# Moving the column term of three tiles from VectorE to GpSimd and one rounding of W from ScalarE to VectorE

## The chip, the cores and the metric

The kernel runs on one core of one Trainium2 chip. The metric is the device time of one execution in microseconds (us); lower is better. The core has five engines with instruction queues of their own: TensorE (PE: matrix products, with its weight loads shown as PEld), VectorE (DVE), ScalarE (ACT), GpSimd (POOL) and SyncE (SP), which issues nearly all the DMAs. Each engine takes its own queue in order; they meet at semaphores.

## The reference

The input x is (2, 512, 1024) and the context is (2, 1024, 1024), both float32. Cut to what matters:

```python
def fake_quant(x, s, z):                       # 8 bits, range 0..255
    return (clip(round(x / s + z), 0, 255) - z) * s

x = x + matmul(fake_quant(layernorm(x), s1, z1), fake_quant(ctx, s2, z2))
n = layernorm(x).reshape(-1, 1024)             # 1024 rows
probs = softmax(n @ W_router.T)                # 8 experts
topk_p, topk_i = top_k(probs, 2); topk_p /= sum(topk_p)
h = einsum('nd,erd->ner', n, A_stack) * combine(topk_p, topk_i)   # rank 16 each
x = x + n @ W_base.T + b_base + einsum('ner,eor->no', h, B_stack) * 2
```

## The kernel before, in words

The 1024 rows of x are eight tiles of 128 rows (`T` = 8), tiles 0 to 3 from the first batch and 4 to 7 from the second (`TB` = 4). A tile lies in `xs[:, t, :]` as 128 partitions by 1024 float32, and is changed in place through the whole kernel.

First stage, per tile: VectorE takes the mean and variance of x (`statistics_x`), GpSimd makes the scale and the bias of the quantisation (`scale_x`; VectorE itself for tile 0), VectorE writes the quantised bytes (`quantise_x`, L556). TensorE transposes them (L825), VectorE copies them back (`take_a1t`, L561), and TensorE multiplies with the quantised context (`product`, L840), which ScalarE makes chunk by chunk as the context's DMAs land (L366). Since the bytes carry an offset, the product needs a correction that depends on the column alone, the column term `corr`. TensorE sums the columns of the context (L831), ScalarE turns them into `corr` (`make_corr`, L371, one for each batch). VectorE adds the product to xs (`sum_x1`, L573), and then the column term (`add_corr`, L506, two inputs of 128x1024 in SBUF).

Second stage, per tile: VectorE takes the statistics of the sum (`statistics_y`, L510, L513, L514), GpSimd makes `y_scale` and `y_bias` (`scale_y`, six small operations, L293 to L323), and the normalised rows y are made: for tile 0 by VectorE (`make_first_y`, L518), for tile 1 by GpSimd (`make_y`, L329), for the others by ScalarE. y is kept as a float16 high part and a float16 rest. W is split the same way: its scale comes from its largest magnitude, which ScalarE finds chunk by chunk (L401), VectorE spreads onto a diagonal (`spread_w_peaks`, L581, L582), TensorE spreads over the partitions (L920, after product k = 4 of tile 3), and VectorE turns into `scale_w` (`make_w_scale`, L587, L588, L590). Then ScalarE makes the high parts of the eight chunks of W in order (`split_w`, L412, after which come the high part of y's tile 1 and other splits), and VectorE the low parts (L625). The low part of chunk k frees the slot of the staging ring into which SyncE loads the context chunk 8 + k of the second batch (`load_ctx`, L207, L208).

TensorE's order in the second stage is written out by hand. After product k = 1 of tile 3 it transposes y of tile 0 (L856), after k = 4 comes the spreading of the peaks. Then come the products of tiles 0 and 1 with W's high parts chunk by chunk as they are ready (L889), those with the low parts, the narrow products for the router and A (L868 to L870), the column sums of the second batch with the transposition of the gated values `hc` of tile 1 after its chunk 3 (L862), and the last product of tile 1 (`lora`, L877), which waits for `hct_lo` (`split_hct`, L682). From tile 2 on each tile is narrow products, products with W, the first-stage product of tile t + 2, and `lora`.

VectorE's order is a written list too. Around the change it is, with tiles in brackets: sum (0), quantise (2), (3), copy back (2), column term (0), statistics (0), copy back (3), sum (1), diagonal of A's peaks, y (0), column term (1), statistics (1) with the diagonal of W's peaks between the halves, the scales, the low halves of y (0), sums (2), (3), W's low parts. Near tile 1's gate it is: gate (1), quantise (4), bias (0) (`add_bias`, L691), `hct_lo` (1), output sum (0) (`sum_out`, L697), column term (3).

GpSimd's list is short: fills, `scale_x(1, 2)`, `scale_x(2, 4)`, `scale_y(0)`, `scale_y(1)`, `make_y(1)`, `scale_y(2)` and so on.

Of the kernel before, what the change touches and what calls it, by code (L numbers as in the profile page):

```python
# [6 lines left out]
ALU = mybir.AluOpType  # L7
# [23 lines left out]
def xattn_ffn(nc, x, ctx_kv, quant, w_t, bias, ar_t, b_t, out):  # L31
# [13 lines left out]
    TB = T // B  # L45
# [7 lines left out]
    with ExitStack() as stack:  # L53
# [3 lines left out]
        def sem(name):  # L57
            return stack.enter_context(nc.semaphore(name))

        xs = sb("xs", [P, T, D], F32)  # L60
        stage = sb("stage", [P, RING, D], F32)
# [3 lines left out]
        corr = sb("corr", [P, B, D], F32)  # L65
        bias_sb = sb("bias_sb", [P, D], F32)
        b_raw = sb("b_raw", [P, D], F32)
        w_hi = sb("w_hi", [P, K, D], F16)
# [68 lines left out]
        def ar_bank(t):  # L137
            return 3 if t == 1 else 2

        COLSUM_BANK = 6  # L140
        WARM_BANK = 5
        PEAK_BANK = 4
# [18 lines left out]
        ctx_ready = sem("ctx_ready")  # L161
        stage1_done, x1_summed = sem("stage1_done"), sem("x1_summed")
        colsum_done, corr_ready = sem("colsum_done"), sem("corr_ready")
        x1_ready = sem("x1_ready")
        rows_summed = sem("rows_summed")
        floor_set = sem("floor_set")
        w_peaks, w_diag_ready, peaks_spread, w_scale_ready = (sem(n) for n in ("w_peaks", "w_diag_ready",
# [1 line left out]
        ar_peaks, ar_diag_ready, ar_peaks_read, ar_scale_ready = (  # L169
            sem(n) for n in ("ar_peaks", "ar_diag_ready", "ar_peaks_read", "ar_scale_ready"))  # L170
        ar_hi_ready, ar_lo_ready = sem("ar_hi_ready"), sem("ar_lo_ready")
        w_hi_ready, w_lo_ready = sem("w_hi_ready"), sem("w_lo_ready")
        b_hi_ready, b_lo_ready = sem("b_hi_ready"), sem("b_lo_ready")
        y_measured, pool_step = sem("y_measured"), sem("pool_step")
        y_scaled, y_ready, y_transposed = sem("y_scaled"), sem("y_ready"), sem("y_transposed")
# [12 lines left out]

        def w_staged(k):
            return stage_in[k], 32  # L190

        def yt_hi_landed(t):
            return yt_hi_in[t % 2], 16 * (t // 2)
# [84 lines left out]
        @block.gpsimd  # L278
        def _(pool):
            def fill(tile):  # L280
                return nc.gpsimd.memset(tile.rearrange("p t d -> p (t d)").bitcast(U32), OFFSET_PAIR)

            steps = [0]

            def then(ins):
                steps[0] += 1
                ins.then_inc(pool_step, 1)
                pool.wait_ge(pool_step, steps[0])

            def inverse_root(mv, t):  # L290
                w = slice(t, t + 1)
                whole, guess, part = root[:, 0, w], root[:, 1, w], root[:, 2, w]
                then(nc.gpsimd.tensor_scalar(whole, mv[:, w, 1], EPS, None, ALU.add))  # L293
                then(nc.gpsimd.tensor_tensor(guess, whole, minus_half[:, w], ALU.pow))
                then(nc.gpsimd.tensor_scalar(part, whole, guess, guess, ALU.mult, ALU.mult))
                then(nc.gpsimd.tensor_scalar(part, part, -0.5, 1.5, ALU.mult, ALU.add))
                return guess, part

            def inverse_roots(mv, w):
                whole, guess, part = root[:, 0, w], root[:, 1, w], root[:, 2, w]  # L300
                then(nc.gpsimd.tensor_scalar(whole, mv[:, w, 1], EPS, None, ALU.add))
                then(nc.gpsimd.tensor_tensor(guess, whole, minus_half[:, w], ALU.pow))
                then(nc.gpsimd.tensor_tensor(part, whole, guess, ALU.mult))
                then(nc.gpsimd.tensor_tensor(part, part, guess, ALU.mult))
                then(nc.gpsimd.tensor_scalar(part, part, -0.5, 1.5, ALU.mult, ALU.add))
                then(nc.gpsimd.tensor_tensor(guess, guess, part, ALU.mult))
                return guess

            def scale_x(first, last):
                w = slice(first, last)  # L310
                pool.wait_ge(x_measured, last)
                inverse = inverse_roots(mvx, w)
                then(nc.gpsimd.tensor_scalar(q_scale[:, w], inverse, inv_s[:, 0:1], None, ALU.mult))
                then(nc.gpsimd.tensor_tensor(root[:, 2, w], mvx[:, w, 0], q_scale[:, w], ALU.mult))
                nc.gpsimd.tensor_scalar(q_bias[:, w], root[:, 2, w], -1.0, prm[:, 1:2], ALU.mult,
                                        ALU.add).then_inc(x_scaled, last - first)

            def scale_y(t):
                w = slice(t, t + 1)
                pool.wait_ge(y_measured, t + 1)  # L320
                guess, part = inverse_root(mvy, t)
                then(nc.gpsimd.tensor_scalar(y_scale[:, w], guess, part, Y_SCALE, ALU.mult, ALU.mult))
                nc.gpsimd.tensor_scalar(y_bias[:, w], mvy[:, w, 0], y_scale[:, w], -1.0, ALU.mult,  # L323
                                        ALU.mult).then_inc(y_scaled, 1)

            def make_y(t):
                pool.wait_ge(y_scaled, t + 1)
                pool.wait_ge(y_transposed, t)
                nc.gpsimd.tensor_scalar(y[:, :], xs[:, t, :], y_scale[:, t:t + 1], y_bias[:, t:t + 1], ALU.mult,  # L329
                                        ALU.add).then_inc(y_ready, 1)  # L330

            nc.gpsimd.memset(ident[:, :], 0.0).then_inc(ident_ready, 1)
            pool.wait_ge(ident_ready, 1)
            nc.gpsimd.affine_select(out=ident[:, :], in_=ident[:, :], compare_op=ALU.not_equal, fill=1.0,
                                    base=0, pattern=[[-1, P]], channel_multiplier=1).then_inc(ident_ready, 1)
            then(nc.gpsimd.memset(minus_half[:, :], -0.5))
            fill(a2[:, 4:8, :]).then_inc(a2_filled, 1)
            nc.gpsimd.iota(expert_i[:, :], pattern=[[1, EX]], base=0, channel_multiplier=0).then_inc(iota_ready, 1)
            fill(a1[:, 4:8, :]).then_inc(a1_rest_filled, 1)
            pool.wait_ge(consts_ready, 1)  # L340
            scale_x(1, 2)
            scale_x(2, 4)
            scale_y(0)
            scale_y(1)
            make_y(1)
            scale_y(2)
            scale_x(4, 5)
            scale_y(3)
            for t in range(2, T - 1):
                if t >= 3:  # L350
                    scale_y(t + 1)
                if t + 3 < T:
                    scale_x(t + 3, t + 4)

        @block.scalar
        def _(act):
# [53 lines left out]
            def split_w(k):  # L410
                act.wait_ge(w_scale_ready, 1)
                nc.scalar.activation(w_hi[:, k, :], stage[:, k, :], ACT.Identity,  # L412
                                     scale=scale_w[:, 0:1]).then_inc(w_hi_ready, 1)
# [51 lines left out]
                peak_of_w(k)  # L465
            split_first_yt()
            for k in range(K):
                split_w(k)
            split_yt(1)
            split_ar()  # L470
            split_b()
# [23 lines left out]
        def _(dve):  # L495
# [7 lines left out]
            def add_corr(t):  # L503
                dve.wait_ge(x1_summed, t + 1)
                dve.wait_ge(corr_ready, t // TB + 1)
                nc.vector.tensor_tensor(xs[:, t, :], xs[:, t, :], corr[:, t // TB, :], ALU.add).then_inc(x1_ready, 1)  # L506
                dve.wait_ge(x1_ready, t + 1)

            def first_half_y(t):
                nc.vector.bn_stats(bny[:, t, 0, :], xs[:, t, 0:H])  # L510

            def second_half_y(t):
# [57 lines left out]
            def sum_x1(t):  # L570
                dve.wait_ge(stage1_done, t + 1)
                dve.wait_ge(x_quantised, t + 1)
                nc.vector.scalar_tensor_tensor(  # L573
                    out=xs[:, t, :].rearrange("p (h n) -> p h n", h=NH),
                    in0=ps[:, s1_bank(t):s1_bank(t) + 2, :], scalar=s12,
                    in1=xs[:, t, :].rearrange("p (h n) -> p h n", h=NH),
                    op0=ALU.mult, op1=ALU.add).then_inc(x1_summed, 1)
# [43 lines left out]
                                                   op0=ALU.mult, op1=ALU.subtract).then_inc(ar_lo_ready, 1)  # L621

            def split_w(k):
                dve.wait_ge(w_hi_ready, k + 1)
                nc.vector.scalar_tensor_tensor(out=w_lo[:, k, :], in0=stage[:, k, :], scalar=scale_w[:, 0:1],  # L625
                                               in1=w_hi[:, k, :], op0=ALU.mult,
                                               op1=ALU.subtract).then_inc(w_lo_ready, 1)

            def split_b():
                dve.wait_ge(b_hi_ready, 1)  # L630
# [115 lines left out]
            sum_x1(1)  # L746
            spread_ar_peaks()
            make_first_y()
            add_corr(1)
            first_half_y(1)  # L750
            dve.wait_ge(floor_set, 1)
            spread_w_peaks()
# [3 lines left out]
            split_first_yt()  # L756
            sum_x1(2)
            sum_x1(3)
            for k in range(4):
                split_w(k)  # L760
            split_yt(1)
            split_w(4)
# [1 line left out]
            for k in range(5, K):  # L764
                split_w(k)
            make_undo()
            add_corr(2)
            statistics_y(2)
            gate_tile(0)
            split_b()  # L770
# [2 lines left out]
            make_y_lo(2)  # L773
            gate_tile(1)
            quantise_x(4)
            add_bias(0)
            split_hct(1)
            sum_out(0)
            add_corr(3)
            statistics_y(3)  # L780
            centre_a1t(4)
            gate_tile(2)
# [31 lines left out]
        def _(pe):  # L814
# [108 lines left out]

            pe.wait_ge(ar_peaks_read, 1)
            for k in range(K):
                pe.wait_ge(w_hi_ready, k + 1)
                wide(0, k, False, parts=(0,))
                if k == 0:
                    pe.wait_ge(first_half_lo, 1)
                wide(0, k, False, parts=(2,))  # L930
                if k == 2:
                    pe.wait_ge(yt_lo_ready, 1)
                    transpose_y(1)
# [79 lines left out]
```

## Time and profile before

| | us |
|---|---|
| median of 3 runs (lowest, highest) | 168.48 (168.28, 168.65) |
| profiled execution: its own time | 168.88 |
| profiled execution: span of the trace | 167.1 |
| busy: PE / DVE / ACT / POOL | 155.1 / 127.4 / 72.6 / 37.9 |

The span runs from the first instruction to the last; the profiled execution's own time is 1.8 us longer. PE is busy in 93% of the span. A matmul is pipelined: one of 512 columns is shown with 0.38 us, but in a row of them the next starts 0.216 us later, so that a stall of PE is better read from the starts than from the idle time. A group "x6" in a timeline is six instructions from the first one's start to the last one's end.

### The profile page before, as it was taken

To read this page: it belongs to the slowest core of one execution; us is meant where nothing else is said; L and a number is where in the kernel's file an instruction comes from. 1 tells how busy PE (TensorE), PEld (TensorE's weight loads), DVE (VectorE), ACT (ScalarE), POOL (GpSimd) and SP (SyncE) were. 2 spreads that over 40 slices of the span, in tenths; PEclk is the share of its full clock that TensorE was granted. 3 is DMA by queue.
4 is the path that set the end of the run, shared out by engine and by line. 5 is a ranking of instruction groups with operands and counts; after the bars stand their busy time and mean duration, and the time that the engine had idled before them with its cause. 6 is when DMAs were issued, how large, how long until landed. Compare 5 with 4: busy or idle time off the path is not lost.

```text
span 167.1 us, 2467 instructions
## 1 busy us (share of the span) xinstructions
PE 155.1 (93%) x875; PEld 80.5 (48%) x875; DVE 127.4 (76%) x283; ACT 72.6 (43%) x96; POOL 37.9 (23%) x113
## 2 busy tenths in 40 slices
PE   6858889879999999999999999999999999999990
PEld 3324335425446654644564456445644564555540
DVE  7988668999999989999889875988485828607702
ACT  3266699869999873225005300800080008003000
POOL 8204150343000433040614153125300040000000
PEclk9999999999999999999999999999999999999998
DMA  5999999991798523605430903291327002700311
GB/s 100 367 418 409 412 409 408 408 410 63 218 330 263 201 52 74 177 16 158 95 63 4 234 17 63 48 173 34 63 46 205 4 0 44 209 0 0 129 63 65
DMA packets 23677, 26.94 MB, mean 161 GB/s; under 512 B 17776, under 2 KB 18032, under 8 KB 23664
## 3 DMA queue, kind: packets, MB, share of 16 engines
q1 hardware_dynamic: 23520, 26.78, 50.8%
q8 instruction: 7, 0.11, 0.3%
q14 instruction: 6, 0.05, 0.1%
q10 hardware_dynamic: 144, 0.00, 0.0%
HBM read 18.38 MB, written 4.19 MB: 135 GB/s over the span
## 4 chain that ended last, share of the span: by engine, by line
PE 60%; DVE 12%; DMA 10%; ACT 9%; SPq 3%; issue 2%; POOL 2%; DVEq 0%; POOLq 0%
PE ps L889 37%; PE ps L840 10%; DMA xs<-in_x 7%; PE ps L877 6%; ACT w_hi L412 5%; DMA stage<-in_ctx_kv 3%; DVE w_lo L625 2%; SPq L208 2%; PE ps L868 2%; PE ps L870 2%; PE ps L869 2%; ACT a L366 1%; DVE a L556 1%; DVE ar_lo L619 1%; SPq L203 1%
## 5 line engine op out<-in xcount | busy, mean ns | idle before, releaser
L889 PE MATMUL ps<-w_hi,yt_hi 128*128 128x512 f16 x128 | 38.3, 380 | 0.9 <-ACT w_hi L412 0.9
L889 PE MATMUL ps<-w_hi,yt_lo 128*128 128x512 f16 x128 | 38.2, 379 | 0.0
L889 PE MATMUL ps<-w_lo,yt_hi 128*128 128x512 f16 x128 | 37.2, 379 | 0.0
L840 PE MATMUL ps<-a,a_t 128*128 128x512 f16 x128 | 30.1, 379 | 2.2 <-ACT a L366 0.9
L366 ACT ACTIVATE a<-stage,prm,inv_s 128x1024 uint8<-128x1024 f32 x16 | 19.5, 1241 | 9.5 <-DMA stage<-in_ctx_kv 9.2
L447 ACT ACTIVATE gate<-gate,ar_undo 128x1 f32<-128x1 f32 x8 | 2.4, 295 | 46.5 <-DVE gate L661 46.5
L840 PEld LDWEIGHTS ps<-a,a_t 128*128 128x128 f16 x128 | 12.2, 98 | 16.8 <-ACT a L366 1.4
L889 PEld LDWEIGHTS ps<-w_hi,yt_lo 128*128 128x128 f16 x128 | 12.5, 98 | 15.1 <-DVE yt_lo L638 0.2
L889 PEld LDWEIGHTS ps<-w_lo,yt_hi 128*128 128x128 f16 x128 | 12.5, 98 | 14.1
L889 PEld LDWEIGHTS ps<-w_hi,yt_hi 128*128 128x128 f16 x128 | 11.5, 98 | 15.0 <-issue 2.1
L293 POOL TENSOR_SCALAR root<-mvy 128x1 f32<-128x1 f32 x8 | 1.9, 234 | 57.7 <-DVE mvy L514 57.7
L573 DVE SCALAR_TENSOR_TENSOR xs<-ps,con,xs 128x1024 f32<-128x1024 f32 x8 | 10.1, 1275 | 3.7 <-PE ps L840 3.7
L868 PE MATMUL ps<-ar_hi,yt_hi 128*128 128x136 f16 x64 | 11.7, 223 | 0.0
L869 PE MATMUL ps<-ar_lo,yt_hi 128*128 128x136 f16 x64 | 11.7, 223 | 0.0
L870 PE MATMUL ps<-ar_hi,yt_lo 128*128 128x136 f16 x64 | 11.7, 223 | 0.0
L660 DVE MAX8 top<-ps 128x8 f32<-128x8 f32 x8 | 1.3, 166 | 13.6 <-PE ps L870 13.6
L451 ACT ACTIVATE hct_hi<-ps 128x128 fp32r<-128x128 f32 x8 | 2.2, 277 | 19.2 <-PE ps L862 19.2
L691 DVE SCALAR_TENSOR_TENSOR xs<-xs,row_term,bias_sb 128x1024 f32<-128x1024 f32 x8 | 10.3, 1284 | 0.3
L831 PE MATMUL ps<-a,ones 128*128 128x512 f16 x32 | 8.6, 380 | 1.4 <-ACT a L366 1.4
L625 DVE SCALAR_TENSOR_TENSOR w_lo<-stage,scale_w,w_hi 128x1024 f16<-128x1024 f32 x8 | 9.8, 1278 | 0.0
L506 DVE TENSOR_TENSOR xs<-xs,corr 128x1024 f32<-128x1024 f32 x8 | 9.7, 1218 | 0.0
L697 DVE SCALAR_TENSOR_TENSOR xs<-ps,con,xs 128x1024 f32<-128x1024 f32 x7 | 8.9, 1277 | 0.1
(138 smaller groups left out, 248.1 us busy)
## 6 DMA issues: line engine op xcount, KB each, us to landing
stage<-in_ctx_kv SPq DMA_DIRECT2D x16, 512.0 KB, 5.5
stage<-in_w_t SPq DMA_DIRECT2D x8, 512.0 KB, 13.0
xs<-in_x SPq DMA_DIRECT2D x7, 512.0 KB, 12.0
out_dram<-xs SPq DMA_DIRECT2D x7, 512.0 KB, 3.0
ar_raw<-in_ar_t SPq DMA_DIRECT2D x1, 544.0 KB, 13.7
xs<-in_x SPq DMA_DIRECT2D x2, 256.0 KB, 3.8
b_raw<-in_b_t SPq DMA_DIRECT2D x1, 512.0 KB, 12.5
bias_sb<-in_bias SPq DMA_DIRECT2D x1, 512.0 KB, 13.3
```

What stands on the lines that cost most here:

```text
L366: nc.scalar.activation(low_bytes(a2[:, n % K, :]), stage[:, n % RING, :], ACT.Identity, bias=prm[:, 3:4], scale=inv_s[:, 2:3]).then_inc(ct ...
L506: nc.vector.tensor_tensor(xs[:, t, :], xs[:, t, :], corr[:, t // TB, :], ALU.add).then_inc(x1_ready, 1)
L573: nc.vector.scalar_tensor_tensor(out=xs[:, t, :].rearrange("p (h n) -> p h n", h=NH), in0=ps[:, s1_bank(t):s1_bank(t) + 2, :], scalar=s12, ...
L625: nc.vector.scalar_tensor_tensor(out=w_lo[:, k, :], in0=stage[:, k, :], scalar=scale_w[:, 0:1], in1=w_hi[:, k, :], op0=ALU.mult, op1=ALU.s ...
L691: nc.vector.scalar_tensor_tensor(out=xs[:, t, :], in0=xs[:, t, :], scalar=row_term[:, t:t + 1], in1=bias_sb[:, :], op0=ALU.add, op1=ALU.ad ...
L697: nc.vector.scalar_tensor_tensor(out=xs[:, t, :].rearrange("p (h n) -> p h n", n=H), in0=ps[:, OUT_BANK[t % 2]:OUT_BANK[t % 2] + NH, :], s ...
L840: last = nc.tensor.matmul(ps[:, s1_bank(t) + h, :], a1_t[:, t % 4, k, :], a2[:, k, h * H:(h + 1) * H], start=k == 0, stop=k == K - 1)
L868: nc.tensor.matmul(dst, yt_hi[:, p, k, :], ar_hi[:, k, :], start=k == 0, stop=False)
L869: nc.tensor.matmul(dst, yt_hi[:, p, k, :], ar_lo[:, k, :], start=False, stop=False)
L870: last = nc.tensor.matmul(dst, yt_lo[:, p, k, :], ar_hi[:, k, :], start=False, stop=k == K - 1)
L877: ins = nc.tensor.matmul(ps[:, OUT_BANK[t % 2] + h, :], part[:, :], rhs[:, h * H:(h + 1) * H], start=False, stop=stop and part is hct_lo)
L889: ins = nc.tensor.matmul(ps[:, OUT_BANK[p] + h, :], part, rhs[:, k, h * H:(h + 1) * H], start=k == 0 and i == 0, stop=stop and i == 2)
```

## The change

Three things are changed. GpSimd adds the column term of tiles 1, 2 and 3 (`correct_x`), to x itself, after the tile is quantised and before VectorE adds the product; VectorE's `add_corr` for those tiles goes, and its sums of them wait for the addition. VectorE makes the high part of W's chunk 6 (`round_w`) between the low parts of chunks 1 and 2, and ScalarE leaves that chunk out. In VectorE's list `split_hct(1)` stands ahead of `add_bias(0)`.

```diff
+        def w_hi_made(k):
+            if k == VECTOR_W:                      # VECTOR_W = 6
+                return vector_w_hi_ready, 1
+            return w_hi_ready, k + 1 if k < VECTOR_W else k
...
+            def correct_x(t):                      # GpSimd
+                pool.wait_ge(corr_ready, 1)
+                pool.wait_ge(x_quantised, t + 1)
+                nc.gpsimd.tensor_tensor(xs[:, t, :], xs[:, t, :], corr[:, 0, :], ALU.add).then_inc(x_corrected, 1)
...
             scale_x(2, 4)
+            correct_x(1)
+            correct_x(2)
             scale_y(0)
+            correct_x(3)
             scale_y(1)
             make_y(1)
...
             for k in range(K):                     # ScalarE
-                split_w(k)
+                if k != VECTOR_W:
+                    split_w(k)
...
             def first_half_y(t):                   # VectorE from here on
+                if 0 < t < TB:
+                    dve.wait_ge(x1_summed, t + 1)
...
             def sum_x1(t):
                 dve.wait_ge(stage1_done, t + 1)
                 dve.wait_ge(x_quantised, t + 1)
+                if 0 < t < TB:
+                    dve.wait_ge(x_corrected, t)
...
             def split_w(k):
-                dve.wait_ge(w_hi_ready, k + 1)
+                dve.wait_ge(*w_hi_made(k))
...
+            def round_w(k):
+                dve.wait_ge(w_scale_ready, 1)
+                nc.vector.tensor_scalar(w_hi[:, k, :], stage[:, k, :], scale_w[:, 0:1], None,
+                                        ALU.mult).then_inc(vector_w_hi_ready, 1)
...
             make_first_y()
-            add_corr(1)
             first_half_y(1)
...
-            for k in range(4):
+            for k in range(2):
+                split_w(k)
+            round_w(VECTOR_W)
+            for k in range(2, 4):
                 split_w(k)
...
             make_undo()
-            add_corr(2)
             statistics_y(2)
...
             quantise_x(4)
+            split_hct(1)
             add_bias(0)
-            split_hct(1)
             sum_out(0)
-            add_corr(3)
             statistics_y(3)
...
-                pe.wait_ge(w_hi_ready, k + 1)      # TensorE, products with W's high parts
+                pe.wait_ge(*w_hi_made(k))
```

## Rows read from the trace of the kernel before

**Rows 1.** Windows by stage: window, length, busy time by engine, clock, DMA, GB/s.
```profile
32.00:38.00 6.00, 5.06 (x27) 2.34 (x25) 5.73 (x17) 4.43 (x8) 2.01 (x7) 1.00 1.02 406
62.00:70.00 8.00, 7.62 (x42) 4.28 (x41) 7.64 (x19) 2.82 (x5) 2.28 (x7) 1.00 0.49 97
70.00:160.00 90.00, 90.00 (x518) 47.94 (x516) 64.41 (x144) 21.20 (x34) 18.91 (x57) 1.00 0.34 82
...
165.00:167.00 2.00, 0.00 (x0) 0.00 (x0) 0.00 (x0) 0.00 (x0) 0.00 (x0) 0.81 0.22 70
```
**Rows 2.** The chain that ended last: start, us, what.
```profile
31.55 0.72 DVE y L518
...
35.89 8.43 ACT w_hi L412 x8
...
51.48 5.14 DMA stage<-in_ctx_kv
...
67.61 0.21 DVE hct_lo L682
```
**Rows 3.** Timeline of PE: start, us, engine, line, operation, out<-in, count, idle time.
```profile
32.33 1.09 PE L856 MATMUL ps<-ident,y 128*128 128x128 f32 x8
...
34.63 0.32 PE L920 MATMUL ps<-diag,ones_b 128*128 128x384 bf16 x1
...
59.97 2.32 PE L889 MATMUL ps<-w_lo,yt_hi 128*128 128x512 f16 x10
...
63.53 1.90 PE L831 MATMUL ps<-a,ones 128*128 128x512 f16 x8
65.45 0.33 PE L862 MATMUL ps<-ident,hc 128*128 128x128 f32 x1
65.61 1.89 PE L831 MATMUL ps<-a,ones 128*128 128x512 f16 x8
...
69.37 0.23 PE L868 MATMUL ps<-ar_hi,yt_hi 128*128 128x136 f16 x1
```
**Rows 4.** Timeline of VectorE from the quantisation of tile 2 on.
```profile
23.85 1.54 DVE L556 TENSOR_SCALAR a<-xs,q_scale,q_bias 128x1024 uint8<-128x1024 f32 x2 [0.46 <-POOL q_bias L315]
...
26.05 1.22 DVE L506 TENSOR_TENSOR xs<-xs,corr 128x1024 f32<-128x1024 f32 x1
...
28.62 0.21 DVE L514 BATCH_NORM_AGGREGATE mvy<-bny 128x2 f32<-128x12 f32 x1
...
31.46 0.81 DVE L518 TENSOR_SCALAR y<-xs,y_scale,y_bias 128x1024 f32<-128x1024 f32 x1
...
34.23 0.25 DVE L582 TENSOR_SCALAR diag<-ident,top_w 128x128 bf16<-128x128 f16 x1
...
35.25 0.24 DVE L587 TENSOR_REDUCE power<-ps 128x1 f32<-128x128 f32 x1
```
**Rows 5.** Timeline of GpSimd over the same stretch.
```profile
28.92 0.22 POOL L293 TENSOR_SCALAR root<-mvy 128x1 f32<-128x1 f32 x1 [5.10 <-DVE mvy L514]
...
30.97 0.26 POOL L323 TENSOR_SCALAR y_bias<-mvy,y_scale 128x1 f32<-128x1 f32 x1
...
37.83 1.19 POOL L329 TENSOR_SCALAR y<-xs,y_scale,y_bias 128x1024 f32<-128x1024 f32 x1
```
**Rows 6.** Timeline of ScalarE: the column term of the first batch.
```profile
22.82 1.19 ACT L371 ACTIVATE corr<-ps,con 128x1024 f32<-128x1024 f32 x1
```
**Rows 7.** Timelines of VectorE and GpSimd where the two overlap elsewhere.
```profile
61.68 1.23 DVE L655 TENSOR_TENSOR y_lo<-y,y_hi 128x1024 f16<-128x1024 f32 x1 [0.61 <-ACT y L431]
...
61.94 1.01 POOL L303 TENSOR_TENSOR root<-root 128x1 f32<-128x1 f32 x1
...
114.08 1.32 POOL L315 TENSOR_SCALAR q_bias<-root,prm 128x1 f32<-128x1 f32 x1
```
**Rows 8.** Timelines of VectorE and GpSimd at the start: a cast beside a fill.
```profile
1.57 1.80 POOL L281 MEMSET a<- 128x2048 uint32 x1
...
2.39 1.07 DVE L709 CAST ident<-ident 128x128 f16<-128x128 f32 x1
```

More of the change, by code:

```diff
@@ L138, in ar_bank @@
             return 3 if t == 1 else 2
+        VECTOR_W = 6
         COLSUM_BANK = 6
@@ L163, in xattn_ffn @@
         colsum_done, corr_ready = sem("colsum_done"), sem("corr_ready")
-        x1_ready = sem("x1_ready")
+        x1_ready, x_corrected = sem("x1_ready"), sem("x_corrected")
         rows_summed = sem("rows_summed")
@@ L171, in xattn_ffn @@
         ar_hi_ready, ar_lo_ready = sem("ar_hi_ready"), sem("ar_lo_ready")
-        w_hi_ready, w_lo_ready = sem("w_hi_ready"), sem("w_lo_ready")
+        w_hi_ready, vector_w_hi_ready, w_lo_ready = sem("w_hi_ready"), sem("vector_w_hi_ready"), sem("w_lo_ready")
         b_hi_ready, b_lo_ready = sem("b_hi_ready"), sem("b_lo_ready")
@@ L506, in add_corr @@
                 nc.vector.tensor_tensor(xs[:, t, :], xs[:, t, :], corr[:, t // TB, :], ALU.add).then_inc(x1_ready, 1)
-                dve.wait_ge(x1_ready, t + 1)
+                dve.wait_ge(x1_ready, 1 if t == 0 else t - 2)
             def first_half_y(t):
+                if 0 < t < TB:
+                    dve.wait_ge(x1_summed, t + 1)
                 nc.vector.bn_stats(bny[:, t, 0, :], xs[:, t, 0:H])
```

## The prediction

> **What bounds the kernel now.** I read the windows by stage first [rows 1]. From 70 us to 160 us TensorE is busy in all of 90.00 us at clock 1.00: nothing that frees VectorE can shorten that stretch, and whatever happens earlier only moves its beginning. The time to win or lose lies before 70 us: TensorE has 5.06 us of work in the 6 us from 32 to 38, and 7.62 us in the 8 us from 62 to 70. The chain of waits says who sets these two [rows 2]: y of tile 0 on VectorE, then the high parts of W on ScalarE from 35.89, then a context load that starts at 51.48 when a low part of W has freed its slot, and at last `hct_lo` of tile 1 at 67.61, for which TensorE's `lora` waits.
>
> TensorE's timeline gives the size of the last stall [rows 3]. Before `lora` of tile 0 the last of ten matmuls starts at 59.97 + 9 x 0.216 = 61.91, and the next operation after `lora` starts at 63.53: 1.62 us without a stall. (0.216 is the spacing in a row of matmuls: eight take 1.89 and one is shown with 0.38, so (1.89 - 0.38) / 7.) For tile 1 the last of eight starts at 65.61 + 7 x 0.216 = 67.12 and the next operation at 69.37, which is 2.25 us. So 0.63 us are lost there.
>
> The early chain is read from VectorE's and GpSimd's timelines together [rows 4, 5]. VectorE adds the column term of tile 0 at 26.05 and ends its statistics at 28.83; GpSimd, idle for 5.10 us, makes the scale from 28.92 to 31.23; y of tile 0 is made from 31.46; TensorE transposes it at 32.33 and spreads W's peak at 34.63, which ends at 34.95 [rows 3]; VectorE comes to read it at 35.25.
>
> **The change part by part.**
>
> *The addition on GpSimd.* It takes three additions of 1.22 us [rows 4] off VectorE and gives GpSimd three of the same shape. The trace has no GpSimd addition of this size. The nearest row is its one-input operation on 128x1024, 1.19 us [rows 5]; that is the low end. Twice that, 2.38, is the high end, if both inputs come through one interface after the other. Between them: a small GpSimd operation of the same kind takes 0.26 [rows 5], so 0.93 of the 1.19 is for elements, and with two inputs 0.26 + 2 x 0.93 = 2.1 us. I take 2.1, because the next rows speak for one interface that even VectorE's second input goes through.
>
> The Trainium skill's "GPSIMD Engine Reference", section 3.1, gives 4497 ns for a GpSimd addition of 2048 float32, about twice VectorE's; halved, an estimate of 2.25 us. By it the sum below would be 4.05 instead of 3.6 us.
>
> Where do these additions lie? By the clock alone they fit: the column term is ready at 24.01 [rows 6], and two additions of 2.1 end at 28.2, before GpSimd is wanted at 28.92. But beside them VectorE runs the quantisations of tiles 2 and 3 (23.85 to 25.39) and tile 0's addition. Where VectorE runs an operation with two inputs from SBUF, a GpSimd operation stands still until it is over: a small one of 0.19 us takes 1.01 us beside `y_lo` [rows 7], ending at 62.95 when VectorE's ends at 62.91; one of 0.27 us takes 1.32 us at 114.08; there are four such in the trace. The other direction shows once, less cleanly: a cast of 128x128 on VectorE, 1.07 us where an operation of that size takes 0.25 [rows 4], starts during GpSimd's fill and ends at 3.46, just after the fill's end at 3.37 [rows 8]. I take it that each engine holds the other for a whole instruction.
>
> The Trainium skill's "SBUF — State Buffer", section "Who interferes with whom", says the same as a rule: a VectorE operation with two SBUF inputs, or in a mode that uses both ports, and a GpSimd operation exclude each other, and the second to start blocks fully. The four GpSimd rows agree; that VectorE is held by an addition no row of before shows. Without the rule the sum would be that of the first rival.
>
> With 2.1 us the early chain then goes so. GpSimd's first addition gets in after the quantisations, 25.4 to 27.5. VectorE's addition for tile 0, due at 26.05, waits until 27.5 and ends at 28.7; statistics end 2.78 us after its start as before, at 30.3. GpSimd's second addition, which its list puts ahead of `scale_y(0)`, runs from 28.7 to 30.8. Then the scale, 2.31 us, to 33.1. Behind it in GpSimd's queue stands the third addition, ready to start at once, as VectorE's y is; y is a 128x1024 operation of 0.81 us against 1.22 for the addition, so I count it among those that collide. GpSimd needs no message from another engine for its next instruction, so I let it win: 33.1 to 35.2. y starts at 35.2 instead of 31.46: **+3.75 us**. In a formula, 25.4 + 3 x 2.1 + 1.22 + 2.31.
>
> Behind y nothing gives this back except one thing: without tile 1's column term VectorE is no longer late for the peak. It can read it at the end of TensorE's spreading, 0.30 us sooner relative to it, of which a handover takes 0.05: **-0.25 us**. From the scale of W on VectorE works without a break into W's low parts, so the delay goes through to the context load and to `hct_lo`.
>
> What the new waits hold: `sum_x1(1)` waits for the addition of 27.5, before its turn, with everything of VectorE behind it; `sum_x1(2)` and `(3)` have theirs by 35.2, long before theirs. `first_half_y(1)` waits for a sum that is long done: nothing.
>
> *W's chunk 6 on VectorE.* ScalarE's 8.43 us for eight chunks become 7.4 [rows 2]; its next work is then earlier by 1.05 us, but its later work waits for context loads, so nothing comes of it. VectorE pays one more operation ahead of low parts 2 to 7: 0.73 us, the spacing of the two quantisations (1.54 - 0.81) [rows 4]. Low part 6 frees the slot whose load starts at 51.48, and the load lands later by as much: **+0.73 us** in the gate of tile 1, between 0 (if the load has slack) and 0.81. The column terms of tiles 2 and 3 went from places behind that load, or into TensorE's full stretch: nothing from them.
>
> *`hct_lo` ahead of the bias.* The bias of 1.28 us no longer stands between the gate and `hct_lo`: the 0.63 us stall goes, **-0.63 us**. TensorE already waits a little for `hc` of tile 1, from 65.26 (63.53 + 8 x 0.216) to 65.45 [rows 3]; that wait is the one that is late next and takes the 0.73. Tile 0's output sum ends no later than before; its reader, tile 2's product with W, comes only after narrow products of 1.43 us (24 by 0.06).
>
> The sum: 3.75 - 0.25 + 0.73 - 0.63 = **+3.6 us**. On the profiled execution (span 167.1, own time 168.88, so 1.78 us outside the span, untouched) 172.5; on the median, 0.40 lower, 168.48 + 3.6 = **172.1 us**. With GpSimd's addition at 1.19 the statistics become the later of the two and the sum is +1.3 (169.8); at 2.38 it is +4.5 (173.0). If VectorE's y wins the race at 33.1, y is only 1.65 late, and the sum some 1.8 (170.3). If GpSimd gets in between the two quantisations, at 24.66, VectorE loses more: tile 0's addition goes behind both of GpSimd's, y is 5.4 late, the sum +5.25 (173.7).
>
> **The rivals.**
>
> *The additions fit (not slower).* The place is 24.0 to 28.9 us on GpSimd; the price is nothing, as long as `scale_y(0)` starts by 28.92. It holds if the engines don't hold each other for 128x1024 operations, and additions take under (28.92 - 24.01) / 2 = 2.45 us. For it: GpSimd's 5.10 us of idle time; the cast on VectorE may have waited for something else. Against it: four held GpSimd operations. Then the sum is -0.25 + 0.73 - 0.63 = -0.15, 168.3 us; and where the late load has slack, -0.25 - 0.63 = -0.9, 167.6 us.
>
> *Only GpSimd is held.* It adds from 25.4 to 29.6, the scale ends at 31.9, y starts 0.45 late, the peak is read at 35.4, 0.15 late: with the +0.1 of the rest 168.7 us. For it: all clear rows show this direction.
>
> *The clock falls.* In the forecast TensorE stands idle for most of 3.75 us ahead of y's transposes. The clock is 1.00 in every stretch of work, and 0.81 on average in the last two microseconds, when TensorE has stopped [rows 1]. If it fell to its lower level of 1.2 GHz, the 2.30 us from the transposes to the peak would double: 174.4 us. Against it: that row is an idle end, and here some products of tile 3 divide the wait.
>
> **How the numbers follow.** The forecast, with its orders and lengths of the addition, has 0.57 (its own range 169.8 to 173.7); the clock's fall 0.05; only GpSimd held 0.08; the additions fit 0.30, half of it at 168.3 and half at 167.6. A difference under 0.2%, 0.34 us, can't be told from none, so faster means under 168.14, slower over 168.82. Faster: all of the 167.6 and 0.03 of the 168.3 = 0.18. Same: the remaining 0.12 and 0.03 of the one-sided case = 0.15. Slower: 0.57 + 0.05 + 0.05 = 0.67. The range from 168.1 to 174.0 leaves out the 167.6 case (0.15) and the clock (0.05).
>
> **What would show it.** GpSimd's additions: about 2.1 us apart where free, first at 25.4. VectorE's addition of tile 0: 2.7 us long or starting after 27. The scale of tile 0 from 30.8, y from 35.2, TensorE's L856 at 36, ScalarE's first high part at 39.4. `lora` of tile 1 without a stall before it, and a longer one before `hc`'s transposition. The forecast is wrong if VectorE's addition of tile 0 keeps its 1.22 us at 26.05 beside a running GpSimd addition, or if `scale_y(0)` still starts near 28.9.

## The result, and the profile after

The changed kernel takes 174.92 us in the median of 4 runs (174.54 to 175.49), beside 168.56 us (168.28 to 168.99) for the kernel before: a ratio of 1.0378 with a 95% interval of 1.0341 to 1.0414. It is slower by 6.4 us; forecast were 3.6, with a range up to 174.0. The direction holds, and so does the holding of the two engines by each other; the order in which they take turns and the clock of TensorE do not come as forecast.

The profiled execution has a span of 173.7 us and a time of 175.49 us. Its first stage is a little quicker than that of before by chance of the loads: the last operation of `scale_x(2, 4)` ends at 23.20 us instead of 23.82, and times below are compared from that end where it matters. (Of the twelve traces kept, ten have it at 23.05 to 23.32; that of before and that of `third_after_y` have it at 23.82 and 23.84.) Line numbers are those of the changed kernel: L573 is `quantise_x`, L521 the column term, L535 y of tile 0, L601 the diagonal of W's peaks, L606 and L609 the scale of W, L335 GpSimd's addition.

Windows by stage of the changed kernel: window, length, busy time of PE, PEld, DVE, ACT and POOL, clock, DMA share, GB/s.
```profile
24.00:32.00 8.00, 6.02 (x39) 2.88 (x38) 7.93 (x8) 7.12 (x12) 5.25 (x3) 1.00 1.03 406
32.00:34.00 2.00, 0.42 (x2) 0.22 (x3) 1.80 (x4) 1.29 (x4) 1.53 (x5) 1.00 1.03 410
34.00:41.00 7.00, 4.49 (x16) 2.56 (x15) 4.54 (x6) 1.08 (x2) 4.11 (x7) 0.65 0.58 231
41.00:48.00 7.00, 6.77 (x31) 3.04 (x30) 5.82 (x12) 5.29 (x6) 1.46 (x2) 0.87 0.00 1
...
78.00:166.00 88.00, 88.00 (x497) 46.58 (x496) 62.94 (x141) 21.22 (x34) 19.00 (x57) 1.00 0.34 81
```
The full stretch of TensorE is as full as before [rows 1]; it only begins later. What is new is the clock: 0.65 in the mean from 34 to 41 us, where it was 1.00. In windows of 1 us it is 1.00 up to 36 us, 0.50, that is 1.2 of 2.4 GHz, from 37 to 42, and 1.00 again from 43.

VectorE's timeline of the changed kernel; in square brackets, here and below, the idle time before an operation and what ended it.
```profile
23.23 3.58 DVE L573 TENSOR_SCALAR a<-xs,q_scale,q_bias 128x1024 uint8<-128x1024 f32 x2 [0.47 <-POOL q_bias L321]
...
27.39 2.71 DVE L521 TENSOR_TENSOR xs<-xs,corr 128x1024 f32<-128x1024 f32 x1
30.14 0.69 DVE L527 BATCH_NORM_STATS2 bny<-xs 128x6 f32<-128x512 f32 x1
...
34.25 2.81 DVE L535 TENSOR_SCALAR y<-xs,y_scale,y_bias 128x1024 f32<-128x1024 f32 x1 [0.45 <-POOL y_bias L329]
...
42.01 0.29 DVE L606 TENSOR_REDUCE power<-ps 128x1 f32<-128x128 f32 x1 [3.15 <-PE ps L944]
...
42.52 0.15 DVE L609 TENSOR_SCALAR scale_w<-power 128x1 int32<-128x1 int32 x1
```
GpSimd's timeline over the same stretch, and then its addition by line (least, median and longest ns).
```profile
23.46 5.57 POOL L335 TENSOR_TENSOR xs<-xs,corr 128x1024 f32<-128x1024 f32 x2 [0.26 <-ACT corr L385]
31.77 0.22 POOL L299 TENSOR_SCALAR root<-mvy 128x1 f32<-128x1 f32 x1 [2.74 <-DVE mvy L531]
...
34.17 2.34 POOL L335 TENSOR_TENSOR xs<-xs,corr 128x1024 f32<-128x1024 f32 x1
```
```profile
L335 POOL TENSOR_TENSOR xs<-xs,corr x3: 2342/2801/2802, 23.5 to 34.2; 128x1024 f32<-128x1024 f32 x3
```
Read the two against each other. Free, a GpSimd addition takes 2.34 us; the two that meet a quantisation take 2.80. Two quantisations, 1.54 us before [rows 4], take 3.58; tile 0's column term takes 2.71 instead of 1.22 and ends at 30.10, 1.07 us after GpSimd's second addition ends at 29.03; y takes 2.81 instead of 0.81 and ends at 37.06, 0.55 us after the third addition's end at 36.51. The statistics in between (one input) keep their 0.69.

TensorE's timeline of the changed kernel.
```profile
27.53 2.33 PE L864 MATMUL ps<-a,a_t 128*128 128x512 f16 x10 [1.50 <-DVE a_t L578]
...
33.58 1.02 PE L864 MATMUL ps<-a,a_t 128*128 128x512 f16 x4 [1.98 <-issue]
37.12 1.97 PE L880 MATMUL ps<-ident,y 128*128 128x128 f32 x8 [2.52 <-DVE y L535]
38.88 2.77 PE L864 MATMUL ps<-a,a_t 128*128 128x512 f16 x6
41.44 0.53 PE L944 MATMUL ps<-diag,ones_b 128*128 128x384 bf16 x1
...
72.83 0.33 PE L886 MATMUL ps<-ident,hc 128*128 128x128 f32 x1 [0.71 <-DVE hc L699]
73.00 1.89 PE L855 MATMUL ps<-a,ones 128*128 128x512 f16 x8
...
76.12 0.23 PE L892 MATMUL ps<-ar_hi,yt_hi 128*128 128x136 f16 x1
```
The transposes of y, 1.09 us before [rows 3], take 1.97, and six products 2.77 instead of 1.46: the lower clock. From there to 72.83 nothing is new, and `lora` of tile 1 has lost its stall: from the start of the last column sum (73.00 + 7 x 0.216 = 74.51) to 76.12 it is 1.61 us, where it was 2.25. The wait ahead of the transposition of `hc`, by the starts too, is 72.83 - (70.22 + 8 x 0.216) = 0.88 us, where it was 0.19.

From the end of `scale_x` on, in the traces, the sum is: y ends 37.06 - 23.20 = 13.86 us after it, before 32.27 - 23.82 = 8.45, so **+5.41**; from y's end to the end of the spreading of W's peak 41.97 - 37.06 = 4.91 instead of 2.68, **+2.23**; the peak is read 0.04 instead of 0.30 after that, and its reading takes 0.66 instead of 0.60, **-0.20**; from W's scale to tile 2's narrow products 33.45 instead of 33.52, **-0.07**. That is 7.4; the quicker first stage takes 0.6 and the end 0.15 off it, which leaves the 6.6 by which the span grew. The medians differ by 6.4.

### The profile page after: what moved, and what is told of

Same layout as the page of the kernel before. It is cut to its first block, busy times and chain, and to the rows that moved or that the text cites. A ratio compares the mean times of both kernels' runs of the same rounds, so it can differ in the third digit from the quotient of the medians.

```text
span 173.7 us, 2468 instructions
## 1 busy us (share of the span) xinstructions
PE 157.4 (91%) x875; PEld 81.9 (47%) x875; DVE 130.0 (75%) x281; ACT 71.7 (41%) x95; POOL 46.1 (27%) x116
## 4 chain that ended last, share of the span: by engine, by line
PE 59%; DVE 18%; DMA 10%; SPq 3%; issue 3%; ACT 3%; POOL 3%; DVEq 0%; POOLq 0%
PE ps L913 36%; PE ps L864 9%; DMA xs<-in_x 7%; PE ps L901 6%; DVE w_lo L644 5%; DMA stage<-in_ctx_kv 3%; SPq L214 2%; PE ps L892 2%; PE ps L893 2%; PE ps L894 2%; DVE y L535 2%; DVE xs L521 2%; ACT a L380 1%; DVE xs L592 1%; PE ps L880 1%
## 5 line engine op out<-in xcount | busy, mean ns | idle before, releaser
L864 PE MATMUL ps<-a,a_t 128*128 128x512 f16 x128 | 32.1, 396 | 4.2 <-issue 2.0
L592 DVE SCALAR_TENSOR_TENSOR xs<-ps,con,xs 128x1024 f32<-128x1024 f32 x8 | 10.1, 1274 | 4.0 <-PE ps L864 4.0
L573 DVE TENSOR_SCALAR a<-xs,q_scale,q_bias 128x1024 uint8<-128x1024 f32 x8 | 8.5, 1069 | 3.1 <-POOL q_bias L321 3.0
L307 POOL TENSOR_SCALAR root<-mvx 128x1 f32<-128x1 f32 (+1 forms) x6 | 1.4, 229 | 33.4 <-DVE mvx L547 33.4
```

The source lines that it names most:

```text
L573: nc.vector.tensor_scalar(low_bytes(a1[:, t, :]), xs[:, t, :], q_scale[:, t:t + 1], q_bias[:, t:t + 1], ALU.mult, ALU.add).then_inc(x_quan ...
L592: nc.vector.scalar_tensor_tensor(out=xs[:, t, :].rearrange("p (h n) -> p h n", h=NH), in0=ps[:, s1_bank(t):s1_bank(t) + 2, :], scalar=s12, ...
L864: last = nc.tensor.matmul(ps[:, s1_bank(t) + h, :], a1_t[:, t % 4, k, :], a2[:, k, h * H:(h + 1) * H], start=k == 0, stop=k == K - 1)
```

## The experiments

The theory: a GpSimd addition and a VectorE operation that uses the same way into SBUF hold each other for a whole instruction; y of tile 0 is late by that; TensorE's waits let its clock fall; the rest of the change is worth little. The rivals: the new waits on data, GpSimd's queue alone, the rounding on VectorE, or the clock alone. Each ratio is against the kernel before, run beside it (168.60 to 168.76 us).

**Which part costs.** `no_pool_add` is the changed kernel without GpSimd's additions and the waits for them, `pool_add_only` the kernel before with them alone.
```diff
-            correct_x(1)                  # no_pool_add, against the changed kernel
-            correct_x(2)
             scale_y(0)
-            correct_x(3)
...
-                if 0 < t < TB:
-                    dve.wait_ge(x_corrected, t)
...
+            add_corr(1)                   # so too add_corr(2) and add_corr(3), at their old places
```


> The change without GpSimd's additions: VectorE keeps all its column terms, W's chunk 6 is still made by VectorE and hct_lo stands ahead of the bias. My theory (the additions hold VectorE and then let TensorE's clock fall; the rest of the change is worth little): 168.4 us, between 167.9 and 168.7, by +0.73 for the rounding and -0.63 for hct_lo. Rival (the rounding on VectorE or the new order is what costs): above 170.

Measured: 168.47 us, ratio 0.9987 (0.9972 to 1.0001).

```diff
-                if k != VECTOR_W:         # pool_add_only, against the changed kernel
-                    split_w(k)
+                split_w(k)
...
-            round_w(VECTOR_W)
...
+            add_bias(0)
             split_hct(1)
-            add_bias(0)
```


> Only GpSimd's additions, with their waits; W is split by ScalarE alone and hct_lo stays behind the bias. My theory: all of the loss is here, 174.8 us (174 to 175.5), and the clock falls as in the changed kernel. Rival (loss shared with the rounding): 171 to 173.

Measured: 175.45 us, ratio 1.0421 (1.0392 to 1.0449). Windows of its trace:
```profile
32.00:38.00 6.00, 2.06 (x9) 0.74 0.99 394
38.00:46.00 8.00, 7.30 (x27) 0.76 0.02 8
```
(Here PE alone is shown: busy, clock, DMA share, GB/s.) All of the loss is in the additions with their waits, and with them the fall of the clock. Without them the change is worth 0.1 us, which its interval does not tell from nothing.

**Holding, or waiting for data.** In `spare_adds` nothing of the kernel before is taken away and no instruction gets a new operand; only GpSimd adds the column term to itself into a spare tile.
```diff
             scale_x(2, 4)
+            spare_add(1)      # after corr_ready and x_quantised, as correct_x
+            spare_add(2)
             scale_y(0)
+            spare_add(3)      # nc.gpsimd.tensor_tensor(spare[:, t - 1, :], corr[:, 0, :], corr[:, 0, :], ALU.add)
```


> The kernel before, unchanged but for three more additions on GpSimd at the changed kernel's places: the column term plus itself into a spare tile that nobody reads or waits for. No data of the kernel depends on them. My theory (a GpSimd addition holds VectorE's quantisation, addition and y while it runs, and is held by them): the same delays as in the changed kernel, two quantisations in about 3.6 us, tile 0's addition and y of tile 0 at some 2.7 us each, the clock falls, 174.9 us (174.2 to 175.8). Rival (the new waits on data cost the time, and GpSimd's queue ahead of scale_y(0) a little): 168.6 to 169.5, with those operations at 1.54, 1.22 and 0.81 us.

Measured: 174.36 us, ratio 1.0336 (1.0319 to 1.0353). VectorE's timeline in its trace:
```profile
23.27 3.11 DVE L565 TENSOR_SCALAR a<-xs,q_scale,q_bias 128x1024 uint8<-128x1024 f32 x2 [0.46 <-POOL q_bias L316]
...
26.96 2.25 DVE L515 TENSOR_TENSOR xs<-xs,corr 128x1024 f32<-128x1024 f32 x1
...
33.35 2.36 DVE L527 TENSOR_SCALAR y<-xs,y_scale,y_bias 128x1024 f32<-128x1024 f32 x1 [0.44 <-POOL y_bias L324]
```
The same three operations are long, by 1.0 to 1.6 us each, though nothing waits for the sums that GpSimd makes: VectorE is held. The additions themselves are shorter here, 1.89 us free (the same tile is both inputs; why that is quicker was not tried), which fits the smaller loss. The profiled execution, at 172.33 us the quickest of five, kept its clock at 1.00; the other four, 174.0 to 174.7, have mean clocks of 0.977 to 0.99. Whether the clock makes that difference of 1.7 to 2.4 us is not shown: a mean of 0.99 can come from elsewhere, as in the trace of `no_pool_add` (0.989), which has 0.79 from 12 to 20 us and 1.00 from 20 on.

**The third addition and y.**
```diff
             def correct_x(t):
                 pool.wait_ge(corr_ready, 1)
                 pool.wait_ge(x_quantised, t + 1)
+                if t == 3:
+                    pool.wait_ge(y_ready, 1)
```


> The changed kernel, with GpSimd's third addition made to wait until VectorE has made y of tile 0. My theory: y takes 0.81 instead of 2.81 us and all that follows comes 2.0 us earlier: 172.9 us with the clock still at the lower level when y is transposed, 170.6 if it is at 1.00 there (TensorE's waits before tile 2's and tile 3's products are untouched by this). Rival (y is late for another reason): 174.9.

Measured: 172.49 us, ratio 1.0230 (1.0209 to 1.0250). VectorE, then GpSimd, in its trace:
```profile
34.88 0.81 DVE L537 TENSOR_SCALAR y<-xs,y_scale,y_bias 128x1024 f32<-128x1024 f32 x1 [0.44 <-POOL y_bias L329]
35.61 0.69 DVE L529 BATCH_NORM_STATS2 bny<-xs 128x6 f32<-128x512 f32 x1
...
36.39 1.89 DVE L603 TENSOR_SCALAR diag<-ident,top_w 128x128 bf16<-128x128 f16 x1
```
```profile
35.87 2.36 POOL L337 TENSOR_TENSOR xs<-xs,corr 128x1024 f32<-128x1024 f32 x1 [1.02 <-DVE y L537]
```
y is back at 0.81 us. The addition now lies beside two operations of VectorE: the statistics keep their 0.69 us, but the small diagonal of W's peaks, 0.25 us before [rows 4], takes 1.89 and ends at 38.28, just after the addition's end at 38.23. That is the cleanest row for the holding of VectorE. The clock stayed at 1.00 in this trace, though the two earlier waits of TensorE (1.51 and 1.98 us) are there as in the changed kernel. The time lies between my two cases: the clock's loss is gone, but the held diagonal takes some of the gain back. In the trace y ends 35.69 - 23.84 = 11.85 us after `scale_x`, 3.40 late, and from there to the end of the peak's spreading it is 3.06 instead of 2.68, 0.38 more; together 3.8, and the kernel is 3.7 us slower than before. The held diagonal is thus only 0.4 of the 1.9 us above my 170.6. For the rest, 170.6 was reckoned down from the changed kernel's median, which is 1.0 less than the terms of its trace add up to; why that is so stays open.

**The order in GpSimd's queue.**
```diff
+                if t >= 2:
+                    pool.wait_ge(y_ready, 1)
...
             correct_x(1)
+            scale_y(0)
             correct_x(2)
-            scale_y(0)
             correct_x(3)
```


> The changed kernel, with GpSimd's list as first addition, scale_y(0), second and third addition, and both of these waiting until y of tile 0 is made. My theory: tile 0's addition is free again (1.22 us), y comes 1.7 us later than in the kernel before and not 5.4, TensorE has no long wait and the clock stays at 1.00; the diagonal of W's peaks may be held by the second addition for up to 1.5 us, of which 0.4 show: 170.5 us (170.0 to 171.2). Rival (only the clock made the change slow): 168.5.

Measured: 170.75 us, ratio 1.0129 (1.0107 to 1.0150), as expected. VectorE in its trace:
```profile
27.51 1.21 DVE L523 TENSOR_TENSOR xs<-xs,corr 128x1024 f32<-128x1024 f32 x1
...
32.81 0.81 DVE L537 TENSOR_SCALAR y<-xs,y_scale,y_bias 128x1024 f32<-128x1024 f32 x1
...
34.33 1.88 DVE L603 TENSOR_SCALAR diag<-ident,top_w 128x128 bf16<-128x128 f16 x1
```
Tile 0's column term is free as soon as no addition lies beside it. What is left is the first addition between the two quantisations (y 1.85 us late), the held diagonal (0.37), and a wait of TensorE of 0.37 us for y of tile 1, which GpSimd makes after its additions.

**The clock.**
```diff
...
+                if t == 3:
+                    keep_warm(10, PEAK_BANK)         # ahead of tile 3's products
...
                     if t == TB - 1 and k == 1:
+                        keep_warm(14)                # ahead of y's transposes
                         transpose_y(0)
```


> The changed kernel, with idle matmuls on a column of ones in TensorE's two long waits: 10 of 384 columns before the products of tile 3, 14 after its product k = 1, ahead of y's transposes. Their results are not used. My theory: the lower clock from 34.0 to 40.9 us costs what the stretch from y's transposes to the spreading of W's peak grew by (4.85 instead of 2.62 us), so with TensorE kept busy 172.7 us (172.3 to 173.2) and a granted clock of 1.00 from 34 to 41. Rival (the lower clock is beside the path, y's lateness alone costs 6.4 us): 174.9 at clock 1.00.

Measured: 173.20 us, ratio 1.0276 (1.0254 to 1.0298), 1.7 us less than the changed kernel. Windows, then TensorE's timeline, in its trace:
```profile
34.00:41.00 7.00, 6.66 (x38) 3.50 (x36) 5.76 (x12) 1.74 (x3) 4.09 (x8) 1.00 0.57 228
```
```profile
34.37 2.44 PE L841 MATMUL ps<-ones 128*128 128x384 f16 x14
37.06 1.09 PE L880 MATMUL ps<-ident,y 128*128 128x128 f32 x8 [0.25 <-DVE y L535]
37.99 1.46 PE L864 MATMUL ps<-a,a_t 128*128 128x512 f16 x6
39.28 0.33 PE L947 MATMUL ps<-diag,ones_b 128*128 128x384 bf16 x1
```
y's transposes start at the same time as in the changed kernel (37.06 and 37.12), and the spreading 2.16 us sooner. So the lower clock does cost on the path: about what was expected in the trace, and 0.5 us less in the medians. Why the medians show less stays open.

**GpSimd between the quantisations or after them.**
```diff
             def correct_x(t):
                 pool.wait_ge(corr_ready, 1)
-                pool.wait_ge(x_quantised, t + 1)
+                pool.wait_ge(x_quantised, 4)
```


> The changed kernel, with GpSimd's additions all waiting until tile 3 is quantised, which makes the order that the prediction had taken: both quantisations, then the first addition. The trace of the changed kernel has the addition between the two, and y of tile 0 5.4 us late against the end of scale_x. My theory: two quantisations in 1.54 us again, y 25.4 + 3 x 2.34 + 1.22 + 2.31 = 35.95 instead of 31.46, 4.5 us late, so 0.9 us less than the changed kernel: 174.0 us if the clock falls as there, 171.9 if it stays at 1.00. Rival (the order does not matter): 174.9.

Measured: 173.90 us, ratio 1.0329 (1.0295 to 1.0363). VectorE, then TensorE, in its trace:
```profile
23.31 1.54 DVE L573 TENSOR_SCALAR a<-xs,q_scale,q_bias 128x1024 uint8<-128x1024 f32 x2 [0.45 <-POOL q_bias L321]
...
25.51 2.93 DVE L521 TENSOR_TENSOR xs<-xs,corr 128x1024 f32<-128x1024 f32 x1
...
33.21 2.81 DVE L535 TENSOR_SCALAR y<-xs,y_scale,y_bias 128x1024 f32<-128x1024 f32 x1 [1.08 <-POOL y_bias L329]
```
```profile
31.91 1.02 PE L864 MATMUL ps<-a,a_t 128*128 128x512 f16 x4 [1.91 <-issue]
36.08 1.97 PE L880 MATMUL ps<-ident,y 128*128 128x128 f32 x8 [3.15 <-DVE y L535]
```
The prediction's order, made by a wait: y ends 36.02 - 23.28 = 12.74 us after `scale_x`, 4.3 late (4.5 from the formula with the measured length), so 1.1 less than in the changed kernel. The medians show 1.0 us less, but the intervals of the two ratios overlap: it is the trace that speaks against the rival. The clock fell here too, and sooner: it is 0.51 from 33 to 34 us and 0.50 from 34 to 38, and 1.00 again from 40. TensorE has no wait before tile 2's products here, one of 1.91 us before tile 3's, and one of 3.15 before y's transposes.

**The two small parts alone.**
```diff
+            split_hct(1)          # hct_only
             add_bias(0)
-            split_hct(1)
```


> The kernel before, with only hct_lo of tile 1 ahead of tile 0's bias. My theory: TensorE's stall of 0.63 us before lora of tile 1 goes and nothing takes its place: 167.9 us, 0.6 less than before. Rival (the wait moves to tile 0's output sum or to the transposed y of tile 2): within 0.2 us of before.

Measured: 168.45 us, ratio 0.9989 (0.9974 to 1.0004). In its trace the stall is gone, as in the changed kernel: TensorE's timeline has `lora` right behind the column sums.
```profile
65.13 1.89 PE L831 MATMUL ps<-a,ones 128*128 128x512 f16 x8
66.67 0.81 PE L877 MATMUL ps<-b_hi,hct_hi 128*128 128x512 f32 x2
```
That execution took 167.85 us, the quickest of twelve; the slowest took 169.12. Against the trace of before it has gained 0.58 us in the first stage alone (`scale_x` ends at 23.24), and 0.65 from the scale of W to tile 2's narrow products (32.87 instead of 33.52). The medians show 0.15 us, between +0.07 and -0.44, which is not clear of nothing. Why they show less than the 0.65 of the trace stays open: only one trace of this kernel was taken.
```diff
             for k in range(K):                    # w6_only, against the kernel before: ScalarE
-                split_w(k)
+                if k != VECTOR_W:
+                    split_w(k)
...
+            round_w(VECTOR_W)                     # VectorE, between low parts 1 and 2
```


> The kernel before with only the high part of W's chunk 6 made by VectorE. My theory: low part 6 and its context load come 0.73 us later, and with them tile 1's gate and lora: 169.2 us. Rival (the load has slack, or ScalarE's 1.05 us pay for it): 168.6, no difference.

Measured: 168.95 us, ratio 1.0018 (1.0002 to 1.0035): +0.3 us (0.03 to 0.6), about half of what I gave it. In its trace `hc` of tile 1 comes later; by the starts TensorE's wait for it is 65.27 - (63.00 + 8 x 0.216) = 0.54 us, where it was 0.19:
```profile
63.00 1.90 PE L846 MATMUL ps<-a,ones 128*128 128x512 f16 x8
65.27 0.33 PE L877 MATMUL ps<-ident,hc 128*128 128x128 f32 x1 [0.37 <-DVE hc L687]
```

**A version that is faster than both.** If low part 6 is what the gate of tile 1 waits for, something else of VectorE can go behind it.
```diff
-            split_w(4)
-            split_ar()
-            for k in range(5, K):
+            for k in range(4, K - 1):
                 split_w(k)
+            split_ar()
+            split_w(K - 1)
...
+            split_hct(1)
             add_bias(0)
-            split_hct(1)
```


> The kernel before with two exchanges in VectorE's list: hct_lo of tile 1 ahead of tile 0's bias, and the low part of A and the router behind W's low part 6 instead of ahead of 5. No GpSimd addition, no rounding on VectorE. The context load that ends the wait for tile 1's gate starts 1.47 us sooner; TensorE's two waits there (0.63 and 0.19 us) go. My theory: 167.8 us, 0.8 less than before. Rival (as with hct_lo alone, of which the medians kept 0.15 of 0.63): 168.4.

Measured: 168.20 us, ratio 0.9962 (0.9944 to 0.9980), 0.6 us less than before (0.3 to 0.9). VectorE in its trace makes low parts 4 to 6 in a row; TensorE's lines follow:
```profile
45.89 3.67 DVE L625 SCALAR_TENSOR_TENSOR w_lo<-stage,scale_w,w_hi 128x1024 f16<-128x1024 f32 x3
49.47 1.48 DVE L619 SCALAR_TENSOR_TENSOR ar_lo<-ar_raw,scale_ar,ar_hi 128x1024 f16<-128x1024 f32 x2
```
```profile
63.01 1.90 PE L831 MATMUL ps<-a,ones 128*128 128x512 f16 x8
64.94 0.33 PE L862 MATMUL ps<-ident,hc 128*128 128x128 f32 x1
...
68.23 0.23 PE L868 MATMUL ps<-ar_hi,yt_hi 128*128 128x136 f16 x1
```
ScalarE no longer waits for the last context loads there; what it waits for next is TensorE's transposition of tile 0's `hc`. But TensorE's wait for `hc` of tile 1 did not go as expected: it is 64.94 - (63.01 + 8 x 0.216) = 0.20 us, as before. From the scale of W to tile 2's narrow products it is 68.23 - 35.33 = 32.90 us, beside 32.87 in `hct_only`, where ScalarE does not wait for the last loads either. So the traces show the gain of `hct_lo` alone. That the second exchange, of the low parts, is worth anything is not shown: the intervals of the two ratios overlap, and one trace of each kernel cannot tell how often the loads come late.

## Why the prediction was wrong

- **The holding** was right, in both directions, and its place too: tile 0's column term and y collided with additions, and y lost its race with the third one (2.81 us, as in the forecast order). The rivals "the additions fit" and "only GpSimd is held" fall with `spare_adds` and the held diagonal.
- **The length of the addition** was 2.34 us, not 2.1; three of them, 0.7 us. The high end of the range, 2.38, was nearer, and so was the page's halved figure: "GPSIMD Engine Reference" of the Trainium skill, section 3.1, would have given 2.25.
- **The order at the quantisations failed.** I let VectorE's second quantisation follow the first and GpSimd come after both. In the trace GpSimd gets in between, then the quantisation, then GpSimd again, then the column term: the one that stands waiting goes next. I had this order as 173.7 us, y 5.4 late, and measured is y 5.41 late. That these two agree so closely is luck: three additions were 0.7 us longer in all than in that sum, and the held operations ended sooner after their release than by their full lengths (the quantisation 0.55 us after it instead of 0.81, the column term 1.07 instead of 1.22, y 0.55 instead of 0.81). With the order forced to the forecast one y is 4.3 late, 1.1 less.
- **The clock failed by its chance.** It was a rival at 0.05 with a price of 2.3 us, on top of the forecast; the stretch grew by 2.23. With TensorE kept busy the changed kernel takes 1.7 us less. I had put it on the wait before y's transposes, and it is in that wait that it falls in the changed kernel; against it I held that products of tile 3 divide the wait. They do, and do not prevent the fall: in `after_quantise`, in the forecast's own order, they stand between waits of 1.91 and 3.15 us, end at 32.93, and the clock is at its lower level from 33 on. In the changed kernel there are two more waits ahead, 1.50 us before tile 2's products and 1.98 before tile 3's, which I had worked out for VectorE and not for TensorE. What exactly decides is open: `third_after_y` has these two waits and kept 1.00 in its trace, and so did `spare_adds`, with waits of 1.04, 1.51 and 2.06.
- **-0.25 us** for reading the peak came as -0.20. **+0.73** for the rounding is nearly there in the changed kernel's trace, where the wait for `hc` grew by 0.69; alone it measures +0.3. **-0.63** for `hct_lo` is in every trace with it, but the medians of `hct_only` keep 0.15. From the scale of W to tile 2's narrow products the changed kernel has -0.07 against my +0.10 for the two together.
- **A side case** of the sum, that y wins its race with the third addition, has 1.8 us, but 1.65 - 0.25 + 0.10 is 1.5. `third_after_y` shows what could fill the gap: the diagonal that is then held, 0.38 us.

Two steps failed, then. The forecast's order, both quantisations ahead of GpSimd's first addition, gave y 3.75 us late; the changed kernel takes turns and has 5.41. And the sum had no term for the clock, which was weighed as a rival at 0.05 on the ground that products divide the wait; it cost 2.23 us in the trace and 1.7 in the medians. As the clock falls in the forecast's order too, it belonged in the sum and not beside it. By the medians it took both to leave the range: with the clock kept up the time is 173.2, and with the order forced it is 173.9, just inside.

## What to carry to other kernels

GpSimd's idle time beside a busy VectorE is not free: an addition of two SBUF tiles there holds VectorE's operations with two SBUF inputs and its quick one-input ones, and is held by them, so count the lengths of both as one queue. Where that queue delays TensorE, follow its waits as well, since a fall of its clock comes on top. Before work is moved to another engine, see whether something in the same list can go behind the operation that the path waits for: `hct_lo` ahead of the bias took a stall of 0.63 us out of every trace that has it, though the medians of `hct_only` show 0.15 of it, and the kernel with a second exchange, whose own worth is not shown, is 0.6 us quicker than before.

## What was not expected of the hardware

The engine that stands waiting goes next: two quantisations of VectorE issued back to back (1.54 us) let a GpSimd addition in between and took 3.58 us. And holding depends little on size: a 128x128 operation of 0.25 us took 1.89 us beside an addition, while statistics of 512 elements and one input kept 0.69 us beside the same one. Other operations were not held either: in `two_after_y`, beside the third addition, two int32 operations on 128x1 kept 0.15 us and the reading of the peak 0.24, while a float32 operation on 128x2 took 0.54 instead of 0.17 and ended with the addition.
